# A graph network kernel: the second eigenvalue pass with 16 points instead of 64, and a parabola in the last step

## The reference

```python
h = relu(layernorm(x)); x = x + L0(h, adj)   # graph convolutions, then LSTMs over windows of 1 to 4 nodes
h = relu(layernorm(x)); x = x + L1(h, adj)   # graph attention, masked by adj
h = relu(layernorm(x)); x = x + L2(h, adj)   # causal attention, scores + adj
h = relu(layernorm(x)); x = x + L3(h, adj)   # a layer between two products with eigenvectors
```

```python
deg = sum(A, axis=0) + sum(A, axis=1) - diagonal(A)
L_norm = rsqrt(deg)[:, None] * (diag(deg) - A) * rsqrt(deg)[None, :]
_, U = eigh(L_norm)
out = relu(U.T @ features @ W1 + b1) @ W2 + b2
return U @ out
```

## Time and profile before

| what | value |
|---|---|
| runs (median, lowest to highest) | 844.22 us (842.39 to 844.63) |
| profiled execution | 844.66 us, span 842.7 us |
| mean granted clock of TensorE | 0.973 |
| busy: PE, DVE, ACT, POOL | 761.1, 705.9, 496.5, 186.7 us |

### The profile page before, as it was taken

The page is one execution under the profiler, slowest core; times in us unless marked ns, Lnnn a source line. Parts: engine busy times, 40 slices in busy tenths (PEclk is TensorE's granted clock), DMA queues, the critical chain, the costliest instruction groups (busy, mean ns, idle before and its releaser), DMA issues.

```text
span 842.7 us, 13724 instructions
## 1 busy us (share of the span) xinstructions
PE 761.1 (90%) x3731; PEld 509.0 (60%) x3738; DVE 705.9 (84%) x3445; ACT 496.5 (59%) x1115; POOL 186.7 (22%) x387
## 2 busy tenths in 40 slices
PE   4689989999999999999999997589978878797998
PEld 3578864445555666666555555567757656676665
DVE  6888769998888888888888889999899999887533
ACT  0379966674454444444444433469957878697775
POOL 3111112222222221221222122532123413340000
PEclk9999999999999999999999998889999999999999
DMA  9200000000000000000000000000000000000122
GB/s 268 69 2 2 1 1 0 2 1 0 1 1 2 1 1 0 1 1 2 0 1 0 1 1 0 1 1 1 1 0 2 1 1 2 1 1 0 51 75 75
DMA packets 13970, 12.16 MB, mean 14 GB/s; under 512 B 1091, under 2 KB 10822, under 8 KB 13894
## 3 DMA queue, kind: packets, MB, share of 16 engines
q1 hardware_dynamic: 10992, 8.47, 3.4%
q10 hardware_dynamic: 2902, 2.82, 1.1%
HBM read 7.10 MB, written 4.19 MB: 13 GB/s over the span
## 4 chain that ended last, share of the span: by engine, by line
issue 44%; DVE 22%; PE 19%; POOL 11%; ACT 3%; POOLq 0%; DVEq 0%
PE bank L742 17%; POOL col_root L465 7%; POOL XI L469 3%; DVE tt L995 3%; DVE stat L1003 3%; DVE HT L995 3%; DVE X L996 2%; DVE uu L995 2%; ACT T L693 1%; PE bank L752 1%; DVE sm L1144 1%; ACT T L571 1%; DVE wih L995 1%; DVE sm L1140 1%; DVE dm L995 0%
## 5 line engine op out<-in xcount | busy, mean ns | idle before, releaser
L635 ACT ACTIVATE G<-bank,bias 128x512 f32<-128x512 f32 (+1 forms) x252 | 158.2, 633 | 174.4 <-PE bank L742 154.2
L742 PE MATMUL bank<-HT,wih 128*128 128x512 f32 (+1 forms) x504 | 244.9, 574 | 0.4 <-ACT HT L621 0.4
L465 POOL TENSOR_TENSOR col_root<-sa,neg_half 128x1 f32<-128x1 f32 x126 | 69.2, 550 | 400.5 <-DVE sa L997 400.5
L742 PE MATMUL bank<-H,whh 128*128 128x512 f32 (+1 forms) x288 | 136.9, 557 | 1.1 <-DVE H L995 0.8
L575 ACT COPY T<-bank 128x512 f32<-128x512 f32 x138 | 80.4, 586 | 54.7 <-PE bank L742 38.8
L571 ACT ACTIVATE T<-X,nbias,rstd 128x128 f32<-128x128 f32 x256 | 104.4, 484 | 7.1 <-DVE nbias L996 7.1
L742 PEld LDWEIGHTS bank<-HT,wih 128*128 128x128 f32 x504 | 80.5, 192 | 14.6 <-issue 8.1
L742 PEld LDWEIGHTS bank<-VI 128*128 128x128 f32 x254 | 45.3, 195 | 68.1 <-DVE VI L995 52.6
L742 PEld LDWEIGHTS bank<-XI,A 128*128 128x128 f32 x252 | 44.3, 195 | 57.2 <-DVE A L996 47.7
L752 PE MATMUL bank<-ident,T 128*128 128x128 f32 x256 | 40.3, 286 | 34.6 <-ACT T L693 26.8
L628 ACT ACTIVATE T<-C 128x512 f32<-128x512 f32 (+1 forms) x72 | 41.4, 576 | 30.1 <-DVE C L995 29.8
(11 more groups left out here) (357 smaller groups left out, 1654.6 us busy)
## 6 DMA issues: line engine op xcount, KB each, us to landing
out_x<-T SPq DMA_DIRECT2D x16, 256.0 KB, 2.2
wih<-in_WihT ACTq DMA_DIRECT2D x1, 1024.0 KB, 12.2
whh<-in_WhhT ACTq DMA_DIRECT2D x1, 1024.0 KB, 18.0
qkvT<-in_WqkvT ACTq DMA_DIRECT2D x1, 192.0 KB
wg<-in_Wg ACTq DMA_DIRECT2D x2, 64.0 KB
l3w<-in_L3W ACTq DMA_DIRECT2D x2, 64.0 KB
adj<-in_adj SPq DMA_DIRECT2D x1, 64.0 KB, 1.9
adjT<-in_adjT ACTq DMA_DIRECT2D x1, 64.0 KB
```

Of the source, the lines that this page charges most:

```text
L465: e.tensor_tensor(out=col["root"][:, :], in0=sa[:, 0:1], in1=neg_half[:, :], op=ALU.pow).then_inc(root_ready, 1)
L635: e.activation(G[x.h][:, gate, 0:n], gate_bank(k)[:, 0:n], ACT.Tanh if gate == 2 else ACT.Sigmoid, bias=bias[:, 4 * (x.p - 1) + gate:4 * ( ...
L742: mm = lambda out, l, r, start=True, stop=True: e.matmul(out, l, r, start=start, stop=stop)
```

## The change

The second pass has 16 points in an interval and cuts its tables and products into 2 pieces of 8 steps, so a step's operations have 32 columns. The spacing of the points in the interval is 1/15 of its width instead of 1/63. The last step adds the bend: second differences of the determinants, averaged over neighbouring points, picked for the partition's interval, divided by the difference of the two determinants and limited to half. Three rounds of a fixed-point iteration then give the zero of the parabola. With the shorter pieces the planner puts the signs of the second pass's blocks in slots 14, 17, 20 and 22.

```diff
-POINTS = (32, 64)
+POINTS = (32, 16)
-CUTS = ((0, KB // 2, KB), (0, 6, 11, KB))
+CUTS = ((0, KB // 2, KB), (0, KB // 2, KB))
...
-... prodL = ... sb("prodL", [P, KB * 2 * POINTS[-1]])
+... prodL = ... sb("prodL", [P, KB * 2 * max(POINTS)])
...
+                if ps:
+                    dd, s2, w2 = uu[0][:, 0:f], mx[:, 0:f], mx[:, f:2 * f - 1]
+                    link(STT(mx[:, 2 * f:3 * f - 2], dd[:, 1:f - 1], -2.0, dd[:, 0:f - 2], ALU.mult, ALU.add))
+                    link(TT(s2[:, 1:f - 1], mx[:, 2 * f:3 * f - 2], dd[:, 2:f], ALU.add))
+                    link(e.tensor_copy(out=s2[:, 0:f:f - 1], in_=s2[:, 1:f - 1:f - 3]))
+                    link(TT(w2, s2[:, 0:f - 1], s2[:, 1:f], ALU.add))
                 e.wait_ge(sum_ps, NB * (ps + 1))
...
             link.note(dot(tt[:, 0:f], uu[0][:, 0:f], red[:, 0:f], c("d_at")))
+            link.note(dot(tt[:, 2 * f:3 * f - 1], mx[:, f:2 * f - 1], red[:, 0:f - 1], c("bend")))
             link(dot(tt[:, f:2 * f - 1], uu[0][:, 1:f], red[:, 0:f - 1], c("d_up")))
             link(TT(c("d_up"), c("d_at"), c("d_up"), ALU.subtract))
+            link(TS(c("d_up"), c("d_up"), 1e-30, None, ALU.add))
             link(e.reciprocal(out=c("d_up"), in_=c("d_up")))
-            link(TT(c("frac"), c("d_at"), c("d_up"), ALU.mult))
-            link(TS(c("frac"), c("frac"), 0.0, 1.0, ALU.max, ALU.min))
+            link.note(TT(c("frac0"), c("d_at"), c("d_up"), ALU.mult))
+            link(TS(c("bend"), c("bend"), c("d_up"), 0.25, ALU.mult, ALU.mult))
+            link.note(TS(c("frac"), c("frac0"), 0.0, 1.0, ALU.max, ALU.min))
+            link(TS(c("bend"), c("bend"), -0.5, 0.5, ALU.max, ALU.min))
+            for _i in range(3):
+                link(STT(c("turn"), c("frac"), -1.0, c("frac"), ALU.add, ALU.mult))
+                link(STT(c("frac"), c("turn"), c("bend"), c("frac0"), ALU.mult, ALU.add))
+                link(TS(c("frac"), c("frac"), 0.0, 1.0, ALU.max, ALU.min))
             link(TT(c("frac"), c("frac"), c("cnt1"), ALU.add))
```

More of the change, by code:

```diff
@@ L325, in build @@
         col = {n: sb("col_" + n, [P, 1]) for n in (
-            "deg rowsum diag pos inv dinv root signed size a1 q sgm mxe mxd mnd lo w cnt1 frac d_at d_up lam mn idx ss inr lmax sign gcol").split()}
+            "deg rowsum diag pos inv dinv root signed size a1 q sgm mxe mxd mnd lo w cnt1 frac d_at d_up lam mn idx ss inr lmax sign gcol frac0 bend turn").split()}
         Nm, NT, XT, VT, D_, QT, TT_ = [sb(n, [P, P]) for n in "Nm NT XT VT D_ QT TT_".split()]
@@ L334, in build @@
         uu, tt, mx = [sb(f"uu{i}", [P, 128]) for i in range(2)], sb("tt", [P, 128]), sb("mx", [P, 128])
-        below, block_hot, prodL = sb("below", [P, P]), sb("block_hot", [P, P]), sb("prodL", [P, KB * 2 * POINTS[-1]])
+        below, block_hot, prodL = sb("below", [P, P]), sb("block_hot", [P, P]), sb("prodL", [P, KB * 2 * max(POINTS)])
         DLP, N2P, QQ, RQ, t2 = sb("DLP", [P, P, 2]), sb("N2P", [P, P, 2]), sb("QQ", [P, P, 2]), sb("RQ", [P, P, 2]), sb("t2", [P, KB, 2])
```

## The result

The changed kernel takes 823.58 us (median of 4 runs, 820.54 to 825.04), the one before 843.35 us on the same chip: ratio 0.976, 95% interval 0.973 to 0.979, or 19.8 us less.

A forecast was written before the change was run, and what follows sets the result against it. VectorE was taken to bound the second pass, then TensorE and ScalarE's round: 16.3 us less over intervals, 2.85 less before, 3.2 more behind, 0.7 for the clock; 15.2 less, 829.2 us after half the difference to the median, range 825 to 833.

The forecast's parts named there:

- The step: One recurrence step on VectorE in the second pass: 0.455 us at 32 columns, 0.275 less, 17.6 us over 64 steps.
- the start of the pass: Second pass up to output 8 (outputs numbered by attention group): 2.85 us less, from stalls and the smaller points operation.
- the intervals 8 to 9 and 15 to 16: Between those VectorE outputs in the second pass: 8.9 us becomes 6.45, and 9.58 becomes 7.9.
- the added operations: Second differences and the longer last step, on VectorE between outputs 21 and 22: 3.2 us longer.
- stalls by GpSimd: VectorE operations held during GpSimd's table work in the second pass: 5.5 us in the pass, to go with smaller tables.
- I rebuild the intervals with the longer of the two: Outputs 8 to 21: each interval the longer of VectorE's time and the others' round; 77.3 us in place of 93.6.
- The clock term: TensorE slow after idling some 2.4 us in interval 15 to 16: 0.7 us added.
- The slower one: Rival: after output 21 TensorE stays at the lower clock through nine groups, 36 us more, 865 us; chance 0.02.
- The longer round: Rival: second-pass intervals 0.5 us longer in 11 places plus a second slow stretch of 1.5, 836 us; chance 0.14.
- the gain given back behind the pass: Rival: VectorE and GpSimd's vector chain ends last, so the gain is lost before the last mixer; 843 us, chance 0.02.
- All 25 us of VectorE's work: Rival: TensorE and ScalarE's round doesn't hold VectorE back in the second pass, all 25 us come; 820 us, chance 0.05.
- the half-way form of that rival: Half of the gain beyond the round comes, with second-pass intervals of 5.4 and 5.1 us: 825 us; no separate chance.

The follow-up runs named there:

- e12_three: The changed kernel with three pieces (6, 5 and 5 steps) instead of two for the second pass's tables and products, still 16 points: 824.41 us, ratio 0.976.

## Why the prediction was wrong

**What was right.** VectorE set the second pass before and the round of the others sets most of it after; shown for TensorE by the load on TensorE that costs nothing in one kernel and 3.4 us in the other. The step (0.455 forecast, 0.45 measured), the start of the pass (2.85 less forecast, 2.7 measured), the intervals 8 to 9 and 15 to 16, the added operations (3.2 forecast; 3.0 and, by leaving them out, 3.2 measured) and the stretch from output 22 to the end came out as costed. That stalls by GpSimd lie on VectorE's path with 64 points is shown by the kernel with the cuts alone; how the work saved splits into steps and stalls was not measured by itself, only that no first operation of a step is stalled any more: they have a mean of 188 ns, in place of the 371 of the earlier trace rows.

**The step that failed** is in the sum: "I rebuild the intervals with the longer of the two". It gave 77.3 us for the 13 intervals and 74.15 were measured. The round does bind, but it binds TensorE's own timeline, not each interval of VectorE. VectorE takes an output some time after TensorE has made it, and that lateness is a store: it grows in an interval where VectorE has more to do, and is given back in the next ones, which run at VectorE's own 4.6 us while TensorE goes on at its 5.86 or 5.41. TensorE's timeline shows it for outputs 9 and 10 (the products with the values):

```profile
618.36 1.12 PE L742 MATMUL bank<-H,T 128*128 128x128 f32 x8
...
624.75 1.13 PE L742 MATMUL bank<-C,T 128*128 128x128 f32 x8
```

The product of output 9 is done at 619.5 and taken by VectorE at 621.47, 2.0 us late; that of output 10 is done at 625.9 and taken at 626.06, 0.2 late. The 1.8 us between are what the interval of 4.59 gave back. It is the same behind output 16: its product is done at 660.2 and taken at 662.92, 2.7 late, that of output 17 at 667.2 and taken at 667.52, 0.3 late. The program permits it: of VectorE's outputs, TensorE's product with the values of a group waits only for that of two groups before (`earlier`, lines 915 and 932). I had counted the long interval of VectorE in full and then full rounds of TensorE as well; that counts the lateness twice. The terms: 9 to 10 is 1.27 us shorter than in my sum, 16 to 17 0.8, the transition to the second kind of attention (14 to 15, 5.41 for 5.86) 0.45, the rest 0.6; together 3.1. The kernel with the late VectorE shows the mechanism by itself: 1.63 us late, 0.29 left.

Counted rightly, the pass is a chain on TensorE from the product it starts with: the 12 masks from 619.32 to 683.55 are 11 rounds of together 64.2 us. In them it idles longest where VectorE's scores come late (0.75 us and 0.96 us), and otherwise a few tenths at a time, as three times 0.24 us for ScalarE's copies; these lines are in its timeline:

```profile
623.28 0.66 PE L752 MATMUL bank<-ident,T 128*128 128x128 f32 x4 [0.75 <-ACT T L693]
...
664.59 0.66 PE L752 MATMUL bank<-ident,T 128*128 128x128 f32 x4 [0.96 <-ACT T L693]
```

**The clock term**, 0.7 us, was for nothing: after waits of 0.75 and 0.96 us, and after one of 1.82 us at 616.90, TensorE's products keep their length (0.66 for four transposes), and the clock is 1.00 from output 8 to 21. I had forecast 2.4 us of idle time there, by the same double count. Before, three slow stretches lay in the pass. After output 22, where TensorE now waits 7.78 us (4.02 in the earlier trace rows), it is slow for one round and no longer, but three products are slow (1.91, 1.91 and 1.67 us) where before only one was (1.91 in the earlier trace rows). That makes output 22 to 23 6.31 us in place of 5.52; by the end it is made up:

```profile
706.26 1.11 PE L752 MATMUL bank<-ident,T 128*128 128x128 f32 x4 [7.78 <-ACT T L693]
```

**The rivals.** The slower one (the lower clock through nine groups) did not come; from output 22 to 31 it is 51.1 us against 50.4. The rule of the Trainium skill (TensorE: Matmul & The Clock Gate, the section on HAM oscillation) that long gaps are each paid anew agrees with the trace: 7.78 us, and then one slow round. My prediction had stretched it to every idle place, and those of 0.75, 0.96 and 1.82 us were not paid. The longer round did not come, since the plain rounds are 5.86 and 5.41 us as forecast. Nor was the gain given back behind the pass, with 114.0 us from output 22 to the end. All 25 us of VectorE's work did not come either; the half-way form of that rival, 825, was the nearest.

**The range.** The terms 3.1 and 0.7 make 829.2 into 825.4, inside the range. In the profiles they are nearly all of the miss: from the start of the second pass to the end the change gives 19.2 us, where I had forecast 15.2. The remaining 1.8 us to 823.6 are within what the chance ahead of the second pass moves in a few runs: six runs of the changed kernel lie between 820.3 and 826.2. My base of 844.66 was an ordinary one (the median of 56 runs of the kernel before in the later measurements is 844.65), but the four runs beside the changed kernel had 843.35.

## What to carry to other kernels

When an engine stops being the bound, don't take the longer of two durations interval by interval: follow the new bound's own timeline, and ask how late the old one may be before it is felt. The intervals right behind a late place are where the gain is larger than the sum says. Before believing a few microseconds between two profiles, compare a point ahead of the change: here it was 3 to 5 us of chance, and medians of 4 runs carry a part of it.

## What was not expected of the hardware

TensorE's speed in the first layer differs from execution to execution of the same code. Its granted clock from 110 to 160 us is 0.97 or 1.00, worth 1.5 to 1.7 us. Its products reach their short length (eight of them 1.06 us in place of 2.08) at about 41 us in one profile and only at about 51 us in another, worth up to 3.6 us; the granted clock doesn't show all of this, since in the later one (run e12_three) it reads 1.00 from 0 to 100 us all the same. Together they move the start of the first pass between 519.7 and 525.0 us. VectorE operations of 32 columns take 0.19 us each, but two that don't depend on each other start 0.11 us apart, two that do 0.22 to 0.23; so a step of three costs 0.45 and not 0.57. GpSimd's product of two tables of 1024 columns takes 2.36 us and a table of 1024 1.90; with 256 columns they take 0.73 and 0.62.
